# Moving the feed-forward weight loads from the ScalarE DMA queue to the SyncE DMA queue

## Chip, cores and metric

One Trainium2 chip, all 8 cores. Each core runs the same program on its own 2,048 of the 16,384 tokens; nothing is exchanged between cores. The metric is the device time in microseconds of the slowest core.

## What is computed

A transformer layer with attention over the 16 heads of one token, then a feed-forward block with ternary weights. Both blocks are wrapped as x + layernorm(block(layernorm(x))).

```python
def _quantize(w):
    gamma = jnp.mean(jnp.abs(w))
    return jnp.clip(jnp.round(w / (gamma + EPS)), -1.0, 1.0)
# attention: qkv = x @ W_qkv; scores over heads of one token; softmax; @ v; @ W_out + b_out
x = x + _layernorm(attn(_layernorm(x)))
# feed-forward, D = 2048, FF = 5632
x1 = _layernorm(x) @ _quantize(w1).T
x2 = _layernorm(x) @ _quantize(w2).T
hidden = sigmoid(x1) * x2
x = x + _layernorm(hidden @ _quantize(w3).T)
```

## The kernel before

Each core holds 2,048 tokens and works on them in two chunks of C = 1024. In order of time: chunk 0 goes through layernorm, QKV (`_phase_qkv`), attention, output projection (`_phase_wout`) and the residual (`_phase_y_ln_resid`); then chunk 1 does the same while `_quant_step` turns w1, w2 and w3 into ternary bf16 copies in HBM (`qw1T`, `qw2T`, `qw3T`); then `_phase_ffn` runs for chunk 0 and for chunk 1. The change is inside `_phase_ffn`.

The order of work is written out by hand. A `Builder` keeps one instruction list for each of the five sequencers (`sync` is SyncE, `scalar` ScalarE, `tensor` TensorE, `vector` VectorE, `gpsimd` GpSimd). `b.emit(engine, ...)` appends an instruction to that engine's list, and `b.wait_free` and `b.wait_ready` append semaphore waits to it. Each list is executed strictly in order, DMA issues among the rest: a DMA issue stands behind every wait and every instruction that was appended to the same list before it. `wait_free(ring, buffer)` waits until the last reader of the buffer is done, `wait_ready` until its last writer is.

`_phase_ffn` has three parts for each chunk:

- **The w1/w2 part** (lines 1038 to 1123). Twenty-two steps `mc`, each of 256 hidden columns. In a step, `wi = 0` multiplies by a band of w1 and `wi = 1` by a band of w2. A band is 1 MB and is loaded by two DMAs of 512 KB (lines 1070 to 1074). For each `wi` there are 4 groups (`mt`, `sub`) of 16 accumulating matmuls (line 1089), so 64 matmuls a band and 128 a step. After each w1 group ScalarE takes the sigmoid out of PSUM (line 1100); after each w2 group VectorE multiplies sigmoid and PSUM into `hid` (line 1117). w1 groups alternate between PSUM buffers `pbig` 0 and 1, w2 groups between `pbig` 2 and `pscore` 0. In chunk 0 each of w1 and w2 has a single SBUF buffer (`bandw1b` and `bandw2a`, keys `bandS`), since the others are still taken; in chunk 1 each has two (`bandw1a`/`bandw1b`, `bandw2a`/`bandw2b`).
- **The w3 part** (lines 1128 to 1191). Sixteen steps `dc`, each with a band of w3 of 1.4 MB, four DMAs of 352 KB (lines 1145 to 1149) into one half of the double buffer `band3`, then two groups of 44 matmuls (line 1168). `band3` lies over `bandw1a`, `bandw1b` and most of `bandw2b`, so its loads wait until those are no longer read. VectorE casts the result (line 1180) and GpSimd stores it to `yscr`. In chunk 0 at `dc == 1` the token matrix of chunk 1 is fetched by `_ffn_t2f_load`: 16 transposing DMAs on the sync list (line 1001), each waiting for the last w1/w2 matmul of chunk 0.
- **The tail** (lines 1208 to 1250). Eight row tiles: a transposing DMA from `yscr` on the sync list (line 1218), statistics and normalization on VectorE with two small ScalarE activations (lines 391 and 396), the residual (line 1240), and a store from GpSimd. The transposes alternate between two buffers, so from the third on each waits for VectorE to have read the tile two earlier (line 409).

Ahead of the feed-forward of chunk 0 stands `_phase_y_ln_resid(chunk=1)`, built in the same way: eight transposing DMAs on the sync list (line 764), and two layernorms for each tile with their ScalarE activations. `_ffn_t2f_load(0)` stands on the sync list ahead of it.

In the kernel before, all loads of w1, w2 and w3 bands are on the `scalar` list, between the ScalarE activations:

```python
for mc in range(NMC):
    for wi in range(2):
        ring = "scalar"
        ...                       # wait_free / wait_ready on ring, 2 DMAs on ring
        # 4 groups: 16 matmuls on tensor, then for wi == 0 a sigmoid on scalar
```

Of the kernel before, what the change touches and what calls it, by code (L numbers as in the profile page):

```python
# [236 lines left out]
def _build_all(b, ctx):  # L237
# [59 lines left out]
    for chunk in range(2):  # L297
        _phase_ffn(b, ctx, chunk)
        if b.dbg == "of":
            _dump_dram(b, ctx, "yscr", g("yscr")); return  # L300
        if b.dbg == "hid":
            _dump(b, ctx, "hid", g("hid")); return
        if b.dbg == "t2f":
            _dump(b, ctx, "t2f", g("t1f")); return
# [687 lines left out]
def _ffn_t2f_load(b, ctx, chunk):  # L992
    t2f = ctx["t1f"]
    act2 = ctx["act2scr"]
    b.wait_ready("sync", ("act2", chunk, 0))
    b.wait_ready("sync", ("act2", chunk, 1))
    for f in range(KD):
        b.wait_free("sync", ("t1f", f))
        b.emit("sync", lambda e, d=t2f[:, f * C:(f + 1) * C],
               s=act2[chunk * C:(chunk + 1) * C, f * 128:(f + 1) * 128]:  # L1000
               e.dma_start_transpose(out=d, in_=s),
               inc="dTf", inc_k=16)
    setm = ("dTf", b.pc["dTf"])
    for f in range(KD):
        b.produced(("t1f", f), setm)
    b.produced("t2f", setm)


def _phase_ffn(b, ctx, chunk):
# [27 lines left out]
    last_w1w2_mm = None  # L1037
    for mc in range(NMC):
        for wi in range(2):
            ring = "scalar"  # L1040
            if chunk == 0:
                dsem = f"dBS{wi}"
                bkey = ("bandS", wi)
                bandbuf = (ctx["bandw1b"], ctx["bandw2a"])[wi]
            else:
                dsem = f"dB{wi + 1}{mc % 2}"
# [80 lines left out]
    src3 = ctx["qw3T"].rearrange("(k p) m -> p k m", p=128)  # L1127
    for dc in range(NDC):
        b3 = ("band3", dc % 2)
        ring, dsem = (("scalar", "dB3a") if dc % 2 == 0 else ("scalar", "dB3b"))  # L1130
        b.wait_free(ring, b3)
        b.wait_free(ring, ("band", 0, 0))
        b.wait_free(ring, ("band", 0, 1))
        b.wait_free(ring, ("band", 1, 0))
        b.wait_free(ring, ("band", 1, 1))
        b.wait_free(ring, ("bandS", 0))
        b.wait_free(ring, ("ofin", 0))
        b.wait_free(ring, ("ofin", 1))
        b.wait_free(ring, ("xstg", 0))
        b.wait_free(ring, ("xstg", 1))  # L1140
        b.wait_ready(ring, "qwT3_done_0")
        b.wait_ready(ring, "qwT3_done_1")
        base3 = (dc % 2) * MFF * 128
        mlast = None
        for g4 in range(4):
            mlast = b.emit(ring, lambda e,
                           d=band3[:, base3:base3 + MFF * 128].rearrange("p (k m) -> p k m", m=128)[:, g4 * 11:(g4 + 1) * 11, :],
                           s=src3[:, g4 * 11:(g4 + 1) * 11, dc * 128:(dc + 1) * 128]:
                           e.dma_start(out=d, in_=s), inc=dsem, inc_k=16)
        b.produced(b3, mlast)  # L1150
        if chunk == 0 and dc == 1:
            _ffn_t2f_load(b, ctx, 1)
            ctx["_t2f_loaded_1"] = True
        for sub in range(2):
            mg = dc * 2 + sub
            pb = mg % 4
            pbuf = ("pbig", pb)
            b.wait_free("tensor", pbuf)
            b.wait_ready("tensor", b3)
            for k in range(MFF):  # L1160
                b.wait_ready("tensor", ("hid", k))
            mm = None
            for k in range(MFF):
                mm = b.emit("tensor", lambda e, p=pbig[pb][:],
                            w=band3[:, base3 + k * 128:base3 + (k + 1) * 128],
                            r=hid[:, k * C + sub * 512: k * C + sub * 512 + 512],
                            st=(k == 0), sp=(k == MFF - 1):
                            nc.tensor.matmul(p, w, r, start=st, stop=sp),  # L1168
                            inc="sT" if k == MFF - 1 else None)
            b.produced(pbuf, mm)  # L1170
            if sub == 1:
                b.consumed(b3, mm)
            if dc == NDC - 1 and sub == 1:
                for k in range(MFF):
                    b.consumed(("hid", k), mm)
            b.wait_ready("vector", pbuf)
            osl = ("ttok", mg % 2)
            b.wait_free("vector", osl)
            m_e = b.emit("vector", lambda e, d=ttok[:, (mg % 2) * D:(mg % 2) * D + 512],
                         s=pbig[pb][:]: nc.vector.tensor_copy(d, s), inc="sV")  # L1180
            b.consumed(pbuf, m_e)
            b.produced(osl, m_e)
            b.wait_ready("gpsimd", osl)
            b.wait_free("gpsimd", "yscr")
            m_w = b.emit("gpsimd", lambda e,
                         d=yscr[dc * 128:(dc + 1) * 128, sub * 512:sub * 512 + 512],
                         s=ttok[:, (mg % 2) * D:(mg % 2) * D + 512]:
                         e.dma_start(out=d, in_=s), inc="dYw", inc_k=16)  # L1188
            mj = b.join("gpsimd", [m_w])
            b.consumed(osl, mj)  # L1190
            out_wr.append(m_w)
# [101 lines left out]
```

How the kernel before makes its waits and increments, by code:

```python
            def wrapped(e, fn=fn, sem=sem, k=inc_k):  # L62
                fn(e).then_inc(sem, k)
# [7 lines left out]
    def wait(self, eng, sem_name, val):  # L71
        if val is None or val <= 0:
            return
        w = self.waited[eng]
        if w.get(sem_name, 0) >= val:
            return
        w[sem_name] = val
        sem = self.sem(sem_name)
        self.streams[eng].append(lambda e, s=sem, v=val: e.wait_ge(s, v))
        self.meta[eng].append(("w", sem_name, val))
```

## Time and profile before

| | us |
|---|---|
| median of three runs | 4797.99 |
| the three runs | 4756.2, 4797.99, 5081.45 |
| profiled execution, time | 4762.08 |
| profiled execution, span of the slowest core (core 6) | 4760.5 |
| span of the fastest core (core 5) | 4728.0 |
| TensorE matmul busy, share of span | 3069.1 (64%) |
| ScalarE busy | 1060.1 (22%) |
| VectorE busy | 1357.9 (29%) |

The span counts from the core's first to its last instruction. A busy time is the time in which at least one instruction of that engine is running; matmuls overlap, so their single durations are longer than their spacing. The granted clock is a share of 2.4 GHz: 1.00 is the upper level, 0.50 the lower (1.2 GHz). A row of the timeline joins successive instructions of one kind; "x64" says how many, and the bracket says how long the engine had been idle before and what ended that. "SPq" and "ACTq" are the SyncE and ScalarE sequencers issuing DMAs; a DMA row's duration is that of the issue, and the landing time counts from issue to completion.

### The profile page before, as it was taken

The page shows a single profiled execution, that of the slowest core. Times are in us where ns is not written, and L with a number is a line of the kernel's source. Part 1 is how long each engine was busy: PE and PEld are TensorE (multiplying, and loading weights), DVE is VectorE, ACT ScalarE, POOL GpSimd, SP SyncE. Part 2 cuts the span into 40 slices and gives each one's busy share as a digit, 9 for nine tenths or more (in the row PEclk, how much of TensorE's full clock was granted, in tenths as well). Part 3 has the DMA queues.
Part 4 walks back from the last instruction along what each step waited for, and adds up shares of the span by engine and source line. Part 5 has one row for each costly group of instructions (what it writes and reads, how often), then busy time and mean ns, then how long its engine had stood idle before and what let it go on. Part 6 is the DMA issues. An engine that isn't in the chain of part 4 may idle for free.

```text
span 4760.5 us, 41249 instructions; the slowest of 8 cores (4728.0 to 4760.5 us)
## 1 busy us (share of the span) xinstructions
PE 3069.1 (64%) x13836; PEld 1395.3 (29%) x13836; DVE 1357.9 (29%) x2375; ACT 1060.1 (22%) x1189; POOL 596.3 (13%) x1061
## 2 busy tenths in 40 slices
PE   2889611353199812630078888889938788788993
PEld 1333311121144311310033333334413333333441
DVE  3111122213666588755700000000040000000004
ACT  1666655432066623100000000000000000000000
POOL 1111111221033233323100000000000000000000
PEclk9987855676599955865589889989979899888996
DMA  7888744786399776898522222245452222223445
GB/s 144 266 263 263 236 152 151 219 279 201 116 301 299 262 227 199 260 233 230 163 71 53 58 67 53 53 102 103 88 168 53 68 57 53 64 61 65 88 86 159
DMA packets 735120, 718.06 MB, mean 151 GB/s; under 512 B 308160, under 2 KB 619584, under 8 KB 732736
## 3 DMA queue, kind: packets, MB, share of 16 engines
q0 software_dynamic: 120976, 438.37, 28.9%
q10 hardware_dynamic: 368768, 151.02, 13.2%
q1 hardware_dynamic: 245168, 126.03, 10.9%
q8 instruction: 114, 1.87, 0.2%
q14 instruction: 94, 0.77, 0.1%
HBM read 545.43 MB, written 157.29 MB: 148 GB/s over the span
## 4 chain that ended last, share of the span: by engine, by line
PE 49%; DMA 26%; DVE 13%; issue 6%; ACT 3%; SPq 1%; ACTq 1%; DVEq 0%; POOL 0%; POOLq 0%
PE pbig L1089 21%; PE pbig L1168 10%; DMA wsf<-wqkv 8%; PE pbig L530 6%; PE pscore L1089 6%; DMA qw3T<-ttok 5%; DMA wsf<-wout 4%; DMA bandw2a<-qw2T 4%; PE pscore L1168 3%; DVE stats L376 3%; DVE ttok L973 2%; DVE xcst L964 1%; DMA bandw2b<-qw2T 1%; PE pbig L716 1%; DVE xcst L959 1%
## 5 line engine op out<-in xcount | busy, mean ns | idle before, releaser
L530 PE MATMUL pbig<-t1f,wsb 128*128 128x512 bf16 x3072 | 725.5, 401 | 98.8 <-DVE wsb L486 91.1
L1089 PE MATMUL pbig<-t1f,bandw1b 128*128 128x512 bf16 x2112 | 463.2, 380 | 325.6 <-DMA bandw1b<-qw1T 325.6
L1168 PE MATMUL pbig<-hid,band 128*128 128x512 bf16 x2112 | 460.3, 380 | 10.1 <-DMA band<-qw3T 9.1
L530 PEld LDWEIGHTS pbig<-t1f,wsb 128*128 128x128 bf16 x3072 | 310.9, 102 | 513.0 <-issue 234.9
L1089 PE MATMUL pbig<-t1f,bandw2a 128*128 128x512 bf16 x1056 | 305.8, 455 | 205.7 <-DMA bandw2a<-qw2T 205.7
L1100 ACT ACTIVATE sigst<-pbig 128x512 bf16<-128x512 f32 x176 | 105.1, 597 | 1429.2 <-PE pbig L1089 1429.2
L1117 DVE TENSOR_TENSOR hid<-sigst,pbig 128x512 bf16<-128x512 bf16 x88 | 60.5, 687 | 1242.5 <-PE pbig L1089 1242.5
L1089 PEld LDWEIGHTS pbig<-t1f,bandw1b 128*128 128x128 bf16 x2112 | 207.1, 98 | 576.5 <-issue 328.8
L716 PE MATMUL pbig<-t1f,wsb 128*128 128x512 bf16 x1024 | 263.3, 424 | 127.3 <-DVE wsb L486 111.8
L660 PE MATMUL pmix<-wtb,vtb 128*128 128x128 bf16 x256 | 37.4, 300 | 466.8 <-DVE wtb L649 465.1
L1188 POOL DMA_DIRECT2D yscr<-ttok x64 | 34.6, 541 | 2192.1 <-issue 1637.6
L1168 PEld LDWEIGHTS pbig<-hid,band 128*128 128x128 bf16 x2112 | 206.9, 98 | 261.2 <-issue 13.5
L973 DVE TENSOR_TENSOR ttok<-xcst 128x1024 bf16<-128x1024 bf16 (+1 forms) x280 | 185.3, 662 | 255.1 <-DMA qw3T<-ttok 124.5
L1089 PE MATMUL pscore<-t1f,bandw2a 128*128 128x512 bf16 x1056 | 238.7, 379 | 0.0
L1089 PEld LDWEIGHTS pbig<-t1f,bandw2a 128*128 128x128 bf16 x1056 | 116.8, 113 | 389.4 <-issue 311.4
L669 ACT ACTIVATE t1f<-pmix 128x512 bf16<-128x512 f32 x64 | 156.9, 2451 | 324.9 <-PE pmix L660 324.9
L486 DVE CAST wsb<-wsf 128x1024 bf16<-128x1024 f32 x128 | 88.8, 697 | 483.1 <-DMA wsf<-wqkv 399.5
L1089 PE MATMUL pbig<-t1f,bandw1a 128*128 128x512 bf16 x704 | 155.5, 382 | 72.7 <-DMA bandw1a<-qw1T 72.7
L716 PEld LDWEIGHTS pbig<-t1f,wsb 128*128 128x128 bf16 x1024 | 107.5, 107 | 282.4 <-issue 198.6
L391 ACT ACTIVATE lntmp<-mv,epsc 128x1 f32<-128x1 f32 x64 | 18.8, 294 | 723.3 <-DVE mv L382 710.4
L541 ACT ACTIVATE qg<-pbig 128x512 bf16<-128x512 f32 x64 | 150.5, 2358 | 102.7 <-PE pbig L530 102.7
L541 ACT ACTIVATE vg<-pbig 128x512 bf16<-128x512 f32 x64 | 150.3, 2352 | 94.6 <-PE pbig L530 94.6
(89 smaller groups left out, 3155.7 us busy)
## 6 DMA issues: line engine op xcount, KB each, us to landing
xstg<-w POOLq DMA_DIRECT2D x222, 512.0 KB, 6.7
wsf<-w POOLq DMA_DIRECT2D x124, 512.0 KB, 6.2
ttf<-w POOLq DMA_DIRECT2D x100, 512.0 KB, 8.7
wsf<-wqkv SPq DMA_DIRECT2D x192, 256.0 KB, 6.9
band<-qw3T ACTq DMA_DIRECT2D x128, 352.0 KB, 5.8
bandw1b<-qw1T ACTq DMA_DIRECT2D x66, 512.0 KB, 7.0
bandw2a<-qw2T ACTq DMA_DIRECT2D x66, 512.0 KB, 5.0
xcF<-w POOLq DMA_DIRECT2D x50, 512.0 KB, 8.3
```

The costliest lines, as they stand in the source:

```text
L376: s=src_tile_ap[:, j * 512:(j + 1) * 512]: nc.vector.bn_stats(d, s),
L486: nc.vector.tensor_copy(d, s), inc="sV")
L530: nc.tensor.matmul(p, w, r, start=st, stop=sp),
L541: nc.scalar.activation(d, s, AF.Copy, scale=sc), inc="sS")
L669: nc.scalar.activation(d, s, AF.Copy), inc="sS")
L716: nc.tensor.matmul(p, w, r, start=st, stop=sp),
L959: nc.vector.tensor_scalar(d, s_, hg, None, ALU.is_gt), inc="sV")
L973: nc.vector.tensor_sub(d, a, gg), inc="sV")
L1089: nc.tensor.matmul(p, w, r, start=st, stop=sp),
L1100: s=pbig[pb][:]: nc.scalar.activation(d, s, AF.Sigmoid),
L1117: nc.vector.tensor_mul(d, a, p), inc="sV")
L1168: nc.tensor.matmul(p, w, r, start=st, stop=sp),
```

## The change

Every band load of the feed-forward block, w1, w2 and w3, in both chunks, is appended to the `sync` list and no longer to the `scalar` list, together with the waits in front of it. Sizes, buffers, semaphores, the wait conditions and the order of the loads among themselves are unchanged. The position of a load in the whole program text is unchanged too, so on the sync list a load stands behind whatever was appended there earlier: the transposes of lines 764, 1001 and 1218.

```diff
@@ -1037,7 +1037,7 @@
     last_w1w2_mm = None
     for mc in range(NMC):
         for wi in range(2):
-            ring = "scalar"
+            ring = "sync"
             if chunk == 0:
                 dsem = f"dBS{wi}"
                 bkey = ("bandS", wi)
@@ -1127,7 +1127,7 @@
     src3 = ctx["qw3T"].rearrange("(k p) m -> p k m", p=128)
     for dc in range(NDC):
         b3 = ("band3", dc % 2)
-        ring, dsem = (("scalar", "dB3a") if dc % 2 == 0 else ("scalar", "dB3b"))
+        ring, dsem = (("sync", "dB3a") if dc % 2 == 0 else ("sync", "dB3b"))
         b.wait_free(ring, b3)
         b.wait_free(ring, ("band", 0, 0))
         b.wait_free(ring, ("band", 0, 1))
```

## Rows read from the trace of the kernel before

**Rows 1.** Waits, whole span, TensorE at line 1089: total us, times, longest us.

```profile
PE pbig L1089 <- DMA bandw1b<-qw1T: 325.6, 1, 325.6
PE pbig L1089 <- DMA bandw2a<-qw2T: 205.7, 33, 6.9
PE pbig L1089 <- DMA bandw1a<-qw1T: 72.7, 1, 72.7
PE pbig L1089 <- DMA bandw2b<-qw2T: 68.6, 11, 6.5
```

**Rows 2.** Windows of chosen stretches, core 6: busy times, then granted clock, DMA share, GB/s.

```profile
1480.00:1650.00 170.00, 165.28 (x772) 74.55 (x769) 96.66 (x134) 114.92 (x50) 53.40 (x91) 1.00 0.86 292
2393.00:2700.00 307.00, 255.69 (x1088) 110.38 (x1088) 22.00 (x32) 22.78 (x37) 0.00 (x0) 0.90 0.21 56
3190.00:3495.00 305.00, 304.05 (x1408) 137.71 (x1408) 22.11 (x32) 0.00 (x0) 16.76 (x31) 1.00 0.51 108
```

**Rows 3.** Timeline of one w1/w2 step in chunk 0: start us, duration us, what.

```profile
2517.99 0.60 ACT L1100 ACTIVATE sigst<-pbig 128x512 bf16<-128x512 f32 x1 [2.86 <-PE pbig L1089]
2518.07 1.00 ACTq L1074 DMA_DIRECT2D bandw2a<-qw2T  x2
2519.16 2.85 ACTq L1074 DMA_DIRECT2D bandw1b<-qw1T  x2
2524.01 4.96 PE L1089 MATMUL pbig<-t1f,bandw2a 128*128 128x512 bf16 x16 [6.23 <-DMA bandw2a<-qw2T]
...
2539.17 13.98 PE L1089 MATMUL pbig<-t1f,bandw1b 128*128 128x512 bf16 x64
```

**Rows 4.** Timeline at the start of the feed-forward block, chunk 0.

```profile
2336.24 23.75 SPq L764 DMA_TRANSPOSE ytokB<-yscr  x3
...
2384.60 0.20 ACT L396 ACTIVATE rstd<-lntmp 128x1 f32<-128x1 f32 x1
2384.94 1.01 ACTq L1074 DMA_DIRECT2D bandw1b<-qw1T  x2
2392.97 15.98 PE L1089 MATMUL pbig<-t1f,bandw1b 128*128 128x512 bf16 x64 [325.62 <-DMA bandw1b<-qw1T]
2398.67 1.28 ACT L1100 ACT_TABLE_LOAD   x1 [13.87 <-PE pbig L1089]
2415.21 6.44 PE L1089 MATMUL pbig<-t1f,bandw2a 128*128 128x512 bf16 x16 [6.25 <-DMA bandw2a<-qw2T]
```

**Rows 5.** Timeline from the w1/w2 to the w3 part, chunk 0.

```profile
3190.06 25.39 SPq L1001 DMA_TRANSPOSE t1f<-act2scr  x16
3190.93 28.65 PE L1168 MATMUL pbig<-hid,band 128*128 128x512 bf16 x132 [1.01 <-DVE hid L1117]
3219.42 9.66 PE L1168 MATMUL pscore<-hid,band 128*128 128x512 bf16 x44
```

**Rows 6.** Timeline from the tail of chunk 0 to the start of chunk 1.

```profile
3498.70 49.54 SPq L1218 DMA_TRANSPOSE ytokB<-yscr  x8
3558.64 0.20 ACT L396 ACTIVATE rstd<-lntmp 128x1 f32<-128x1 f32 x1
3558.88 1.38 ACTq L1074 DMA_DIRECT2D bandw1a<-qw1T  x2
3567.71 15.71 PE L1089 MATMUL pbig<-t1f,bandw1a 128*128 128x512 bf16 x64 [72.72 <-DMA bandw1a<-qw1T]
```

**Rows 7.** Timeline from the w1/w2 to the w3 part, chunk 1.

```profile
4360.34 3.62 PE L1089 MATMUL pscore<-t1f,bandw2b 128*128 128x512 bf16 x16
4364.10 10.65 ACTq L1149 DMA_DIRECT2D band<-qw3T  x8
4373.06 17.32 PE L1168 MATMUL pbig<-hid,band 128*128 128x512 bf16 x71 [9.10 <-DMA band<-qw3T]
```

**Rows 8.** DMA issues (KB, us to landing); landings and an issue of line 1001.

```profile
wsb<-wqkvb SPq DMA_DIRECT2D x48, 512.0 KB, 5.6
DMA to landing us min/median/max: 3.7/8.4/23.7
2067.48 70.83 SPq L1001 DMA_TRANSPOSE t1f<-act2scr  x16
```

## Prediction

> **What bounds the kernel now.** I read the waits of TensorE first, because it is the busiest engine, then the windows by stage, then the timeline at each place where TensorE stands still in the feed-forward block. The waits show four entries at the w1/w2 matmuls [rows 1]. Two are single and long: 325.6 us before the first band of chunk 0 and 72.7 us before the first of chunk 1. Two are many and short: 33 waits for `bandw2a` and 11 for `bandw2b`, 44 in all, 274.3 us together, so 6.23 us each. There are 22 steps in each chunk, so every w2 band is waited for and, but for the first of a chunk, no w1 band ever is.
>
> The timeline of one step tells why [rows 3]. The two DMAs of the w2 band are issued at 2518.07, 0.08 us after the fourth sigmoid of that step has begun; in the program text that load stands right behind that sigmoid on the scalar list. The w1 matmuls have just ended when the load is issued, and TensorE idles 6.23 us until it lands. The load of the next w1 band follows at 2519.16 and has the whole w2 half to land in, which is why it costs nothing. In chunk 0 the buffer of w2 was free one half step earlier, and in chunk 1 (two buffers) earlier still. So the wait is due to the place in the list, not to a buffer and not to bandwidth: in this stretch the DMA share is 0.21, against 0.86 in the QKV stage [rows 2].
>
> Each stall also costs clock. The granted clock is 0.90 on average in the w1/w2 part and 1.00 in the w3 part, which has no such gaps [rows 2]. Undisturbed, 64 matmuls take 13.8 us: from 2539.17 a row of 64 ends at 2553.15, and the last of them is still in the pipeline when the next could start. By the w3 row, 132 matmuls take from 3190.93 to 3219.42, the next row's start, 28.49 us or 0.2158 us each [rows 5]. So a band is 13.81 us and a step 27.62 us. Measured, chunk 0's w1/w2 part lasts from 2392.97 [rows 4] to 1.01 us before 3190.93 [rows 5], 796.95 us, or 36.22 us a step. The 8.60 us above 27.62 are 6.23 of wait and 2.37 of lower clock after it (2415.21 shows one such group of 16 matmuls, 6.44 us for what takes 3.45 at full clock [rows 4]; 2524.01 a milder one of 4.96 [rows 3]).
>
> **The change, part by part.**
>
> *Steady state of the w1/w2 part.* On the sync list nothing but other loads stands between two band loads. The w2 load of step mc waits for the last w2 matmul of step mc-1 (chunk 0, single buffer) and then has the w1 half of step mc, 13.81 us, to land. Its duration has rows: 2518.07 to 2524.01 is 5.94 us from the first issue to the first matmul [rows 3], and the slowest first load is 2384.94 to 2392.97, 8.03 us [rows 4]. The w1 load likewise gets the w2 half. 13.81 against 5.9 to 8.0 leaves 5.8 us at the least, so both are hidden by matmuls; if that cover went, each would cost 6 us plus 2.4 us of clock, what it costs now. In chunk 1 the two buffers double the room. The SP queue as such is no slower by what rows there are: its 512 KB loads of `wsb` landed in 5.6 us in the median while the DMA engines were at 0.86 [rows 2, 8]. Leaving out the 44 stalls and their clock gives 22 x 8.60 = 189 us in each chunk before edges. What stands next behind the removed wait is TensorE itself: a sigmoid takes 0.60 us for every 3.45 us of matmuls [rows 3].
>
> *ScalarE's list* loses the issues (1.00 and 2.85 us a step [rows 3]) and their waits. Nothing on the path waits for that, so it counts zero; it is spare time of an engine that is busy 22.78 of 307 us [rows 2].
>
> *Start, chunk 0.* Before, the first load stands behind the last activation of the residual phase (2384.60 + 0.20) and is issued at 2384.94 [rows 4]. On the sync list it stands behind the last transpose of line 764, whose issue ends at 2336.24 + 23.75 = 2359.99. With the same 8.0 us the first matmul starts at 2368.0. But two w1 groups fill `pbig` 0 and 1 and the third needs a sigmoid, and ScalarE's sigmoids still stand behind its activation at 2384.60. With the table load of 1.28 and one sigmoid of 0.60 the third group can start at 2384.80 + 1.88 = 2386.7. TensorE is idle from about 2377 to there and falls back to the lower clock, so the third group takes 5.7 us (2392.97 to 2398.67, the first group now [rows 4]) and the fourth 3.45: the w1 half ends at 2395.8. Then w2 follows without a wait, 13.81, then 21 steps of 27.62, 580.0. End at 2989.6, against 3189.92 now: gain 200.3 us.
>
> *w3 part, chunk 0.* Bands 0 and 1 are issued, as now, when the last w1 matmul is done (line 1136), 13.8 us before the part begins; the same two bands took 8.96 us, from 4364.10 to 4373.06, in chunk 1 [rows 7]. Hidden. But band 2 now stands behind the 16 transposes of line 1001, which wait for the last w1/w2 matmul and took 25.39 us to issue [rows 5]. Before, band 2 could be issued after one step of w3, 88 matmuls or 19.0 us, beside the transposes on the other queue. It is needed after two steps, 38.0 us. Now it is issued at 25.4 or later and lands 9 us later at 34.4 (room: 3.6 us). No row shows a load behind transposes on one queue. Lower bound: the transposes go faster alone, nothing lost. Upper bound: the same 16 transposes once took 70.83 us, beside quantization traffic [rows 8]; band 2 would land at 79.8, 41.8 us late, and with 2.4 us of clock cost 44 us. I take 1 us, since the near row is the 25.39, which was itself measured with band 2 under way beside it. Bands 3 to 15 wait for buffers as before and have 19.0 us each.
>
> *Between the chunks.* The first load of chunk 1 is issued at 3558.88 behind the last activation of the tail (3558.64) [rows 6]. On the sync list it stands behind the last transpose, issued by 3498.70 + 49.54 = 3548.24. With the same 8.8 us to the first matmul it gains 10.6 us. ScalarE is done with the tail at 3558.84, before the first group ends (3557.1 + 5.4), so no sigmoid is late here. The load now follows a transpose in its queue, which may cost up to the 3.7 us of the shortest transpose [rows 8]; I take 1 us.
>
> *w1/w2 part, chunk 1.* Now 3567.71 [rows 6] to 4363.96 [rows 7], 796.3 us. After: 22 x 27.62 = 607.6, and the first band's lower clock, 15.71 against 13.98, 1.7 [rows 3, 6], 609.3. Gain 187.0 us.
>
> *w3 part, chunk 1, and tail.* Band 0 overlaps the last w2 band, so the 9.10 us wait [rows 7] stays on either queue. No change.
>
> **Sum.** 200.3 - 1 + 10.6 - 1 + 187.0 = 395.9 us. Against the profiled execution's own 4762.1 us that gives 4366 us. That execution lies 0.75% below the median of the three runs (4798.0) and close to the lowest (4756.2). I forecast the undisturbed time and add 4 us for small joints that I can't see: **4370 us**.
>
> **The rivals.**
>
> *Clock falls under unbroken load* (chance 0.05). After the change TensorE would run some 910 us with hardly a gap (608 + 304), two to three times as long as any such stretch now. The matmuls of the feed-forward block would be 2 x 608 + 2 x 304 = 1824 us at full clock. If the granted clock over it were c, they would take 1824/c: the gain falls under 2% at c = 0.86 and the kernel is 2% slower at c = 0.79. Rows speak against it: 305 us of the w3 part with TensorE busy 304.05 us run at 1.00, and 170 us of the QKV stage, whose operands are dense random numbers, as well [rows 2]. At c = 0.81, about where the time would stand still, it would give 4366 + 428 = 4794 us. The Trainium skill ("TensorE: Matmul & The Clock Gate", Part 1, the note on the peak-current limiter) speaks for this rival: it says that once three cores of a die run dense matmuls the die drops to 13/16 of the clock and that 1.95 GHz should be budgeted for sustained all-core work. An estimate from that page's ratio is 4366 + 1824 x 3/13 = 4787 us. By that rule the w3 part would not stand at 1.00, as it does with all eight cores at work, so the trace disagrees so far.
>
> *Nothing moves* (0.02). All queues feed the same DMA engines, and if the w2 wait were a matter of transfer, not of the place in the list, another queue would not help: 4762 us. Against it stand the issue 0.08 us after the sigmoid and the DMA share of 0.21 [rows 2, 3]. The Trainium skill ("DMA: Bandwidth & Descriptors", section "Issuing engines are not separate DMA queues") states that DMAs started from several engines interleave on the same 16 and that only the sequencer's issue time is saved, usually small. By that sentence alone the 3.85 us a step would leave ScalarE, off the path, and the time would stay at 4762 us; it says nothing of what a load waits behind in its issuer's list, which is what I count.
>
> *Band 2 of w3 is late behind the transposes* (0.08): up to 44 us, so up to 4410 us. For it: the room is only 3.6 us. Against: it happens once, and the 25.39 us has contention in it.
>
> *Loads on the SP queue land too slowly* (0.02; the one that ends slower). Place: every step of chunk 0, single-buffered. If a band takes L us to land, a step takes L + 13.81 + 2.4 as soon as L exceeds 13.81. That equals today's 36.22 at L = 20.0; with chunk 1's gain kept (two buffers give 41 us of room), the whole kernel is slower only when 22 x (L - 20.0) exceeds 197 us, L above 29.0, and by 2% above 33.3. The longest landing on this queue in the trace is 23.7 us, a transpose under heavy traffic [rows 8]. Were both halves of each band to take that, one behind the other, L = 47.4, chunk 0 would lose 22 x 27.4 = 603 us, chunk 1 would gain nothing, and the time would be about 5350 us. Against: 5.6 us in the median for loads of that size on this queue [rows 8].
>
> **How the numbers follow.** My forecast has 0.83, with its own span of 4345 to 4405: the lower end is the start of chunk 0 without the stop for the sigmoid (12 us) and the small terms at zero, the upper end 0.75% above 4370, which is what the median stands above the profiled execution. With late w3 loads on top, the range is 4340 to 4435. What is left out is the rest of 0.09 and part of the joints. About 2% is what a measurement of this kernel can tell from no change. Forecast, late w3 loads and a third of the slower-clock case (a drop to 0.9 only) are faster by over 2%, 0.93; the clock near 0.81 and nothing moved give 0.05 within 2%; 0.02 slower.
>
> **What would show it.** In the profile after: the w2 bands gone from TensorE's waits; the w1/w2 stretches at granted clock 1.00 and 27.6 us a step; first w1/w2 matmul near 2368 with an idle of some 10 us before the third group; w3 of chunk 0 beginning near 2991 and no idle between its steps (an idle of up to 42 us at its third step is the late band); 62 us and not 72.7 between the chunks; 9 us still before the w3 part of chunk 1. The prediction is wrong if w2 waits remain at about 6 us (the list was not the cause), or if the clock column drops under 0.95 in these stretches while TensorE has no gaps.

## Result: faster by 8.1%

The ratio of the changed kernel to the kernel before is 0.919, 95% interval 0.915 to 0.924. Applied to the 4762.1 us of the profiled execution of before that is 4377 us (4356 to 4399); 4370 was forecast. The profiled execution of the changed kernel took 4407.2 us, the lowest run 4373.8 us. In about half of the executions of either kernel a die of the chip runs at a lower clock for much of the time, and since those are left out of the ratio, the median over all ten runs, 4535.9 us, is no measure of the change.

The waits of TensorE in the feed-forward block, changed kernel, core 5 (the slowest): total us, times, longest us.

```profile
PE pbig L1089 <- DVE nbias L402: 285.5, 1, 285.5
PE pbig L1089 <- DMA bandw1a<-qw1T: 65.3, 1, 65.3
PE pbig L1168 <- DMA band<-qw3T: 16.3, 2, 8.9
PE pbig L1089 <- ACT sigst L1100: 9.4, 1, 9.4
```

All 44 waits for w2 bands of [rows 1] are gone. The first row is the wait for the start. VectorE is named as its releaser, but the timeline below shows the first w1 load issued at 2351.36 and the matmuls starting 7.0 us later, so it is that load. New are a wait for a sigmoid, 9.4 us, and a second one for a w3 band.

Windows of the same core: busy times, then granted clock, DMA share, GB/s.

```profile
2420.00:2700.00 280.00, 280.00 (x1299) 126.97 (x1298) 28.18 (x41) 23.92 (x40) 0.00 (x0) 1.00 0.27 76
3650.00:3955.00 305.00, 305.00 (x1415) 138.31 (x1414) 30.24 (x44) 26.31 (x44) 0.00 (x0) 1.00 0.25 70
3980.00:4100.00 120.00, 120.00 (x553) 54.24 (x552) 8.30 (x12) 0.00 (x0) 6.48 (x12) 0.99 0.40 88
4120.00:4320.00 200.00, 200.00 (x763) 82.89 (x762) 11.76 (x17) 0.00 (x0) 9.17 (x17) 0.81 0.31 67
```

TensorE is busy without a gap in the w1/w2 stretches of both chunks, at clock 1.00 where [rows 2] had 0.90. The last row is another matter: in the w3 part of chunk 1 the clock of this core stands at 0.81, below the upper level of 2.4 GHz and well above the lower of 1.2 GHz. More on that below.

The start, and two steps of chunk 0, same core (timeline; rows left out are the residual phase and the rest of the step).

```profile
2348.31 2.84 SPq L764 DMA_TRANSPOSE ytokB<-yscr  x1
2351.36 1.02 SPq L1074 DMA_DIRECT2D bandw1b<-qw1T  x2
...
2358.32 9.65 PE L1089 MATMUL pbig<-t1f,bandw1b 128*128 128x512 bf16 x32 [285.52 <-DVE nbias L402]
...
2374.83 0.20 ACT L396 ACTIVATE rstd<-lntmp 128x1 f32<-128x1 f32 x1
...
2375.18 1.28 ACT L1100 ACT_TABLE_LOAD   x1
...
2377.32 8.70 PE L1089 MATMUL pbig<-t1f,bandw1b 128*128 128x512 bf16 x32 [9.35 <-ACT sigst L1100]
...
2385.86 3.62 PE L1089 MATMUL pbig<-t1f,bandw2a 128*128 128x512 bf16 x16
...
2399.67 13.98 PE L1089 MATMUL pbig<-t1f,bandw1b 128*128 128x512 bf16 x64
2399.97 0.98 SPq L1074 DMA_DIRECT2D bandw2a<-qw2T  x2
...
2413.48 3.62 PE L1089 MATMUL pbig<-t1f,bandw2a 128*128 128x512 bf16 x16
```

The w2 band is now issued at 2399.97, as soon as the w2 matmuls of the step before have ended, and has 13.5 us until it is read at 2413.48. In [rows 3] it was issued after the sigmoids and read 5.9 us later, with TensorE waiting.

### The profile page after: what moved, and what is told of

The parts are those of the page before. It is cut to its first block, busy times and chain, and to the rows that moved or that the text cites. A ratio compares the mean times of both kernels' runs of the same rounds, so it can differ in the third digit from the quotient of the medians.

```text
span 4405.6 us, 41332 instructions; the slowest of 8 cores (4337.8 to 4405.6 us)
## 1 busy us (share of the span) xinstructions
PE 3003.0 (68%) x13836; PEld 1383.5 (31%) x13836; DVE 1356.9 (31%) x2375; ACT 1061.3 (24%) x1189; POOL 596.3 (14%) x1061
## 4 chain that ended last, share of the span: by engine, by line
PE 52%; DMA 22%; DVE 14%; issue 6%; ACT 4%; SPq 1%; DVEq 0%; POOL 0%; ACTq 0%; POOLq 0%
PE pbig L1089 20%; PE pbig L1168 11%; DMA wsf<-wqkv 9%; PE pbig L530 7%; PE pscore L1089 7%; DMA qw3T<-ttok 5%; DMA wsf<-wout 4%; PE pscore L1168 4%; DVE stats L376 3%; DVE ttok L973 2%; DVE xcst L964 1%; PE pbig L716 1%; DVE wsb L486 1%; DVE sums L592 1%; ACT ttf L844 1%
## 5 line engine op out<-in xcount | busy, mean ns | idle before, releaser
L530 PE MATMUL pbig<-t1f,wsb 128*128 128x512 bf16 x3072 | 721.2, 399 | 98.1 <-DVE wsb L486 93.3
L1168 PE MATMUL pbig<-hid,band 128*128 128x512 bf16 x2112 | 491.9, 398 | 16.3 <-DMA band<-qw3T 16.3
L660 PE MATMUL pmix<-wtb,vtb 128*128 128x128 bf16 x256 | 37.4, 300 | 467.6 <-DVE wtb L649 466.0
L716 PE MATMUL pbig<-t1f,wsb 128*128 128x512 bf16 x1024 | 256.0, 414 | 144.2 <-DVE wsb L486 125.0
L1089 PE MATMUL pbig<-t1f,bandw2a 128*128 128x512 bf16 x1056 | 238.7, 379 | 0.0
L1089 PE MATMUL pbig<-t1f,bandw1a 128*128 128x512 bf16 x704 | 156.1, 383 | 65.3 <-DMA bandw1a<-qw1T 65.3
L391 ACT ACTIVATE lntmp<-mv,epsc 128x1 f32<-128x1 f32 x64 | 18.8, 294 | 707.5 <-DVE mv L382 694.2
L1180 DVE CAST ttok<-pbig 128x512 bf16<-128x512 f32 x48 | 33.2, 691 | 472.5 <-PE pbig L1168 472.5
```

## Experiments

All kernels below are edits of one of the two kernels, and each was timed against the kernel before on the same chip.

### The changed kernel once more

> The changed kernel once more, for a second trace. My theory: TensorE's 44 waits for w2 bands are gone and a w1/w2 step takes 27.6 us in both chunks at a granted clock of 1.00; before the w3 part of chunk 0 TensorE waits 7 to 8 us for the first w3 band. The first trace had a granted clock of 0.81 on two cores (4 and 5) in the last 227 us. If that comes of the denser load of the changed kernel, this trace has such a stretch in its feed-forward block too, at some 40 us of cost on a core. If it is chance, it is gone here, and the slowest core is near 4370 us.

Ratio 0.918 (0.912 to 0.925), slowest core 4370.5 us. Windows of that core, core 3:

```profile
2700.00:2966.00 266.00, 266.00 (x1234) 120.54 (x1232) 26.80 (x39) 22.69 (x38) 0.00 (x0) 1.00 0.28 76
3980.00:4280.00 300.00, 297.57 (x1371) 134.60 (x1372) 21.44 (x31) 0.00 (x0) 16.19 (x30) 0.99 0.39 87
```

The w1/w2 part is as in the first trace, and the w3 part of chunk 1 has its clock of 0.99. The stretch at 0.81 is not a fixed part of the changed kernel.

### Is it the queue or the place in the list?

All loads on ScalarE, but those of a step ahead of its sigmoids (compared with the kernel before):

```diff
     for mc in range(NMC):
+        keys = []
         for wi in range(2):
             ring = "scalar"
             ...                      # waits and the two DMAs of the band
             b.produced(bkey, mlast)
+            keys.append((bkey, bandbuf))
+        for wi in range(2):
+            bkey, bandbuf = keys[wi]
             for mt in range(2):      # matmuls, sigmoids, products
```

> All loads stay on the ScalarE list, but the w2 load of a step is put ahead of the four sigmoids of that step. Theory (the place in the list made the stall): w2 waits gone, steps of 27.6 us at clock 1.00; 4762 - 2 x 189 = 4373 to 4385 us, ratio to before about 0.92; start of chunk 0 and the gap between the chunks (72.7 us) unchanged. Rival (the SyncE queue itself is what helped, being faster or empty): the waits of 6.2 us stay, 36.2 us a step, about 4762 us.

Ratio 0.919 (0.916 to 0.921), the same as the change's; lowest run 4385.4 us. One step, timeline of core 5:

```profile
2501.00 13.98 PE L1093 MATMUL pbig<-t1f,bandw1b 128*128 128x512 bf16 x64
2501.30 1.00 ACTq L1075 DMA_DIRECT2D bandw2a<-qw2T  x2
...
2514.81 3.62 PE L1093 MATMUL pbig<-t1f,bandw2a 128*128 128x512 bf16 x16
...
2515.25 1.00 ACTq L1075 DMA_DIRECT2D bandw1b<-qw1T  x2
```

The load is issued at the same point of the step as on SyncE, 0.30 us after the w1 matmuls begin, and TensorE waits for nothing. So the gain does not need the other queue at all. The Trainium skill ("DMA: Bandwidth & Descriptors", section "Issuing engines are not separate DMA queues") says that DMAs share the same 16 engines whichever engine started them, and this case agrees: a second queue brought no more than the first (0.919 both times), and below, a reload on one queue slows the loads on the other. The second rival of the prediction went further and took from that page that nothing would move. It failed, because the place in the list decides when a transfer may begin.

The opposite: loads on SyncE, but each w2 load also waits for the fourth sigmoid of its step.

```diff
+            if wi == 1:
+                b.wait(ring, m_sg[0], m_sg[1])
             src_r = wT[wi].rearrange("(k p) m -> p k m", p=128)
```

> The changed kernel (loads on SyncE), but each w2 load also waits for the fourth sigmoid of its step, which is where the ScalarE list issued it. Theory (only the moment of issue matters): TensorE waits about 6.2 us for each w2 band again, 36.2 us a step, granted clock 0.90; 4370 + 2 x 189 = about 4750 us, less the 20 to 30 us of the earlier starts. Rival (the SyncE queue as such is what helps): the waits stay away or are much shorter than 6 us.

Ratio 1.012 (1.005 to 1.019): the whole gain is gone, and the time is within 2% of that of the kernel before. Timeline of core 0:

```profile
2502.09 0.99 SPq L1076 DMA_DIRECT2D bandw2a<-qw2T  x2
...
2507.91 6.55 PE L1091 MATMUL pbig<-t1f,bandw2a 128*128 128x512 bf16 x16 [6.70 <-DMA bandw2a<-qw2T]
...
2539.52 0.98 SPq L1076 DMA_DIRECT2D bandw2a<-qw2T  x2
```

This step takes 2539.52 - 2502.09 = 37.4 us. From the first w2 group of chunk 0 at 2396.40 to the last but one at 3139.47 there are 20 steps of 37.15 us, against 36.10 in the kernel before (core 6, 21 steps from 2415.21 to 3173.28). The waits are 6.8 and not 6.3 us, since here the load waits until the sigmoid has ended, and in the kernel before it was issued 0.08 us after its start; the other 0.5 us is clock. 44 x 1.05 = 46 us is most of the 72 us that the expectation of 4750 us missed (lowest run 4822 us). The rest lies in the last w2 band of each chunk, same core:

```profile
3170.43 4.49 ACTq L1206 DMA_DIRECT2D xb<-xbscr  x8
3171.04 0.98 SPq L1076 DMA_DIRECT2D bandw2a<-qw2T  x2
...
3189.85 5.23 PE L1091 MATMUL pbig<-t1f,bandw2a 128*128 128x512 bf16 x16 [19.70 <-DMA bandw2a<-qw2T]
```

Held until the last sigmoid, this load starts 0.6 us behind the reloads of the residual `xb` and lands only after 18.8 us; in chunk 1 the wait is 18.6 us. That is 12 to 13 us more than for the other bands, twice. What the reloads do in the changed kernel itself is shown further down. The loads of w2 are on SyncE in this kernel and the stall is back in full, so the moment of issue sets it and not the queue.

### Which loads have to move?

Only the w2 loads on SyncE (compared with the kernel before):

```diff
-            ring = "scalar"
+            ring = "sync" if wi == 1 else "scalar"
```

> The kernel before with the w2 loads alone on SyncE; w1 and w3 loads stay on ScalarE. Theory: the steady state needs no more than this, so 27.6 us a step and 2 x 189 us gained. The start of chunk 0 keeps its place behind the last activation (no gain of 20 us), the gap between the chunks stays 72.7 us, and the xb reload stays behind the w3 loads (no 10 us lost): 4762 - 378 = 4384 us. Rival (w1 loads gained as well in the steady state): the time stays well above, and TensorE waits for w1 bands.

The lowest run was 4388.1 us, against 4757.3 us of the kernel before on the same chip, 0.922. No interval stands behind that, and a second series was run.

> Once more the kernel before with the w2 loads alone on SyncE, since all eight cores of the first trace stood at a granted clock of 0.81 through the whole feed-forward block and no ratio came out. Theory as before: 27.6 us a step, start of chunk 0 and the gap of 72.7 us between the chunks unchanged, 4762 - 378 = 4384 us, ratio about 0.92. Rival (w1 loads gained in the steady state too): clearly above, with TensorE waiting for w1 bands.

Again no interval came out. The lowest run was 4396.0 us, against 4774.4 us of the kernel before on the same chip, 0.921. Waits of core 3, the slowest (4409.8 us):

```profile
PE pbig L1089 <- DMA bandw1b<-qw1T: 313.2, 1, 313.2
PE pbig L1089 <- DMA bandw1a<-qw1T: 75.4, 1, 75.4
PE pbig L1168 <- DMA band<-qw3T: 9.1, 1, 9.1
```

No wait for any band inside the parts is left, though w1 and w3 loads are on ScalarE. The extra w3 wait of the changed kernel is absent. The two edges have not gained: over the eight cores TensorE waits 300 to 313 us at the start (295 to 326 before) and 72.3 to 76.1 us between the chunks (68.9 to 72.7 before, 62.3 to 65.3 in the changed kernel). Moving w2 alone is nearly the whole gain in these times; no interval stands behind the small difference.

### The unforeseen w3 wait

The changed kernel, timeline of core 5, from the w1/w2 to the w3 part of chunk 0:

```profile
2966.46 5.06 ACTq L1204 DMA_DIRECT2D xb<-xbscr  x8
2966.47 23.60 SPq L1149 DMA_DIRECT2D band<-qw3T  x8
...
2987.35 30.75 PE L1168 MATMUL pbig<-hid,band 128*128 128x512 bf16 x132 [7.36 <-DMA band<-qw3T]
2990.64 25.75 SPq L1001 DMA_TRANSPOSE t1f<-act2scr  x16
3016.54 54.63 SPq L1149 DMA_DIRECT2D band<-qw3T  x16
```

In the kernel before, the eight reloads of `xb`, 4 MB, stood on the ScalarE list behind the w3 loads. With those gone, nothing holds them back, and they start within 0.01 us of the first w3 band. The issue of eight w3 DMAs takes 23.60 us, where in [rows 7] it took 10.65. In chunk 1 the reloads start at 3955.62 and the w3 loads, which there have to wait for the last w2 matmul, only at 3969.29; the wait of 9 us for them is that of before. Two runs tell the collision from a fault of SyncE's queue or of the transposes.

```diff
-        ring, dsem = (("sync", "dB3a") if dc % 2 == 0 else ("sync", "dB3b"))
+        ring, dsem = (("scalar", "dB3a") if dc % 2 == 0 else ("scalar", "dB3b"))
```

> The changed kernel with the w3 loads back on the ScalarE list, w1/w2 loads on SyncE. Theory: the 7.4 us wait before the w3 part of chunk 0 comes from the xb reload (8 x 512 KB), which on the ScalarE list no longer stands behind the w3 loads and now shares the DMA engines with the first two w3 bands. With w3 back ahead of it, the wait is gone and about 2 us of lower clock with it: 10 us less than the changed kernel. Rival (the transposes of line 1001 or the SyncE queue are at fault): also gone here, so this run alone does not tell them apart; the run with the xb reload on SyncE does.

```diff
     for i in range(NTT):
-        b.wait_ready("scalar", ("xpark_done", chunk))
-        b.wait_free("scalar", ("xb", i))
-        b.emit("scalar", lambda e, d=xb[:, i * D:(i + 1) * D],
+        b.wait_ready("sync", ("xpark_done", chunk))
+        b.wait_free("sync", ("xb", i))
+        b.emit("sync", lambda e, d=xb[:, i * D:(i + 1) * D],
```

> The changed kernel with the eight xb reloads moved to the SyncE list too, where they stand behind the w3 loads again. Theory (collision with the xb reload): the first w3 wait of chunk 0 falls from 7.4 us to under 1 us with the w3 loads still on SyncE, about 10 us less. Rival (w3 loads are slower on the SyncE queue): the wait of 7.4 us stays.

The first gave 0.915 (0.913 to 0.918), the second 0.914 (0.908 to 0.920). In both, all eight cores have a single w3 wait, that of chunk 1. The second, core 4, its w3 wait:

```profile
PE pbig L1168 <- DMA band<-qw3T: 9.0, 1, 9.0
```

and its timeline at the same place:

```profile
2986.82 12.34 SPq L1149 DMA_DIRECT2D band<-qw3T  x8
...
3000.47 24.38 SPq L1001 DMA_TRANSPOSE t1f<-act2scr  x16
3025.00 14.98 SPq L1149 DMA_DIRECT2D band<-qw3T  x5
```

With the w3 loads still on SyncE, the issue of eight takes 12.34 us again and the wait is gone. So it was the reload beside them. The ratios only agree with that: the cost of the collision, 8.5 us or 0.2%, is less than the width of the intervals, and it is the trace that shows the mechanism.

### Wait and clock, the two terms of the stall

The changed kernel with each w2 load held behind the third sigmoid:

```diff
+            if wi == 1:
+                b.wait(ring, m_sg[0], m_sg[1] - 1)
```

> The changed kernel with each w2 load held back behind the third sigmoid of its step, 3.45 us earlier than behind the fourth. It parts the two terms of the stall, wait and clock. Holding behind the fourth gave waits of 6.7 to 6.8 us. So the wait should be 3.3 us a step. Theory (a wait costs clock in proportion to nothing but its being long enough): if a wait of 3.3 us still costs 2.4 us of lower clock the step is 27.6 + 5.7 = 33.3 us and the time about 4370 + 44 x 5.7 = 4621 us; rival (short waits cost no clock): 30.9 us a step, granted clock 1.00, about 4515 us.

No interval came out. The lowest run was 4631 us (4774 for the kernel before on the same chip), against 4621 expected with a clock cost and 4515 without. Timeline of core 4:

```profile
2547.87 0.98 SPq L1076 DMA_DIRECT2D bandw2a<-qw2T  x2
...
2553.75 6.56 PE L1091 MATMUL pbig<-t1f,bandw2a 128*128 128x512 bf16 x16 [3.32 <-DMA bandw2a<-qw2T]
```

and its window, clock 0.91:

```profile
2500.00:2800.00 300.00, 267.49 (x1114) 115.77 (x1134) 23.80 (x35) 21.53 (x36) 0.00 (x0) 0.91 0.24 64
```

In these rows a wait of 3.3 us is followed by as slow a group of 16 matmuls, 6.56 us, as one of 6.7 us was (6.55). Both rows are near the worst of their kernel, so here are the means: from 2383.59 to 3093.19 this core has 21 steps of 33.79 us, which is 27.62 of matmuls, 3.4 of wait and 2.7 of lower clock. With the waits of 6.8 us above the clock term was 37.15 - 27.62 - 6.77 = 2.8 us, and in the kernel before, with 6.3 us, 2.2 us. Half the wait does not halve the clock term.

### A version that beats both

The largest idle time left is the one before the first w1 band. Most of it is the quantization of w3, which the w1/w2 part does not read.

```diff
-    _quant_step(b, ctx, 10 ** 9)      # ahead of _phase_y_ln_resid(chunk=1)
...
     for mc in range(NMC):
         ...
+        if chunk == 0:
+            _quant_step(b, ctx, 3)
```

(with the `xb` reload on SyncE as above)

> A version that goes further: xb reload on SyncE as before, and the 56 quantization jobs of w3 that are left after the output projection of chunk 1 are no longer done in one piece ahead of the feed-forward block, but three in each w1/w2 step of chunk 0, which does not read w3. With the w2 stalls gone the largest idle time of TensorE is that before the first w1 band, about 285 us. Theory: that idle time shrinks to the residual phase, some 90 us, the w1/w2 steps of chunk 0 stay at 27.6 us since VectorE needs about 7 of them for the three jobs; about 4353 - 300 = 4050 us. Rival: the jobs keep VectorE or the DMA queues so busy that w2 groups wait for their PSUM buffer, steps get longer than 30 us and 50 us or more of it are lost.

Ratio 0.881 (0.877 to 0.885), median 4200 us, lowest 4193 us. The wait before the first w1 band is 111.6 us on the slowest core, core 0, and the w1/w2 part of chunk 0 is as dense as in the changed kernel (the waits, then a window):

```profile
PE pbig L1088 <- DMA bandw1b<-qw1T: 111.6, 1, 111.6
```

```profile
2300.00:2700.00 400.00, 400.00 (x1855) 181.37 (x1854) 129.36 (x186) 35.22 (x59) 49.43 (x88) 1.00 0.55 165
```

VectorE is busy 129 of 400 us there and holds nothing up. The expectation of 4050 us was wrong in its own sum: the idle time could fall only from 285 to some 90 us, which is 195 us and not 300. It fell by 174 us, and the ratio fell from 0.914 (`xb` reload on SyncE alone) to 0.881, 158 us of 4762.

> As the version that quantizes w3 beside the w1/w2 steps of chunk 0, but with all 88 jobs of w3 there, four in each step, and none in the output projection of chunk 1. Theory: the output projection was held up by the jobs (TensorE busy 111.6 of 125 us) and by the queue of their transfers ahead of the residual phase (some 25 us between its last matmul and the first transpose of y); both shrink, 20 to 30 us less than the 4193 us of that version. Rival: four jobs a step are too many for the DMA engines or VectorE, w2 groups wait, and nothing is gained.

This one moved all 88 w3 jobs (four a step) and took them out of the output projection. It has no ratio, and its lowest run was 4252 us. In that execution cores 4 and 5 (4218 and 4250 us) had a granted clock of 0.92 from 3700 to 4000 us; the cores 0 to 3 took 4167 to 4188 us, where they took 4166 to 4195 in the version above. So nothing is gained and little is lost. The start comes sooner (99.9 us of wait on core 0 and not 111.6), but the last jobs now end after the w1/w2 part. On core 0 that part ends at 2786.0, the last store of a w3 job is issued at 2796.66, and the first w3 bands, which wait for it, at 2799.19. TensorE waits some 22 us for them on all eight cores, where it stood idle 1.0 us in the version above (timeline, core 0):

```profile
2808.50 29.99 PE L1167 MATMUL pbig<-hid,band 128*128 128x512 bf16 x132 [22.47 <-DMA band<-qw3T]
```

## Why the prediction was right, point by point

**The cause of the stall** was right, and it is shown from both sides: the same order on ScalarE's own list gives the gain, the old moment of issue on SyncE takes it away.

**Size of the steady state.** 27.62 us a step was forecast. From the first w2 group at 2385.86 to the end of chunk 0's w1/w2 part (2966.02 is the last step's first w2 group) there are 21 steps in 580.2 us, 27.63 each. The cover was a little smaller than the prediction says, since the slowest first load in its rows is 8.83 us ([rows 6]) and not 8.03, but 5.0 us of it were left. Forecast for the whole stretch of chunk 1: 609.3 us; measured from 3358.81 to 3969.17, 610.4 us.

**Start of chunk 0.** All steps of the sum came out, counted from the end of ScalarE's last activation in the residual phase (2384.80 in the forecast, 2375.03 here): first matmul 16.8 us ahead of it (16.7), third group 1.9 us behind it (2.3), first w2 group 11.0 us behind it (10.8).

**The late w3 band 2 behind the transposes.** The transposes took 25.75 us to issue, 25.39 in [rows 5]; the room of 3.6 us held on core 5. On cores 0 and 4 band 2 came 1.8 and 1.0 us late: there the transposes, behind w3 loads that the `xb` reload had slowed, started over 2 us after the w3 matmuls and took 29 us to issue. With the reload out of the way (`xb` on SyncE) they start 0.9 us ahead of the matmuls on core 4, and none of the eight cores waits for band 2. The 44 us of the upper bound did not come.

**Between the chunks.** 62 to 63 us were forecast, 65.3 us measured on core 5 (timeline):

```profile
3348.26 0.98 SPq L1074 DMA_DIRECT2D bandw1a<-qw1T  x2
3349.29 7.34 SPq L1074 DMA_DIRECT2D bandw2a<-qw2T  x2
...
3358.81 16.37 PE L1089 MATMUL pbig<-t1f,bandw1a 128*128 128x512 bf16 x64 [65.27 <-DMA bandw1a<-qw1T]
```

From issue to first matmul is 10.55 us. The forecast had 8.8 from core 6 and 1 more for the transpose ahead, and both were sized wrong. Core 6 was an exception: the other seven took 5.8 to 7.0 us in the kernel before. In the changed kernel all eight took 8.9 to 10.6 us, some 3 us longer in the mean, so that the gap shrank by 6.9 us in the mean (70.2 to 63.3) and not by 9.6. The w2 load one microsecond behind is not what delays it. With w2 held back (the runs behind the third and fourth sigmoid) the w1 load still took 9.7 to 10.4 us on the four cores I read. With all loads on ScalarE's list, where a w2 load follows just as closely but no transposes stand ahead, it took 7.1 and 7.2 us on two cores. Whether it is the queue behind the transposes or the tail's other transfers at that earlier moment, no run separates.

**Missed: the `xb` reload.** The step that failed is "ScalarE's list loses the issues; nothing on the path waits for that, so it counts zero". I looked for what waits for ScalarE and not for what had been waiting behind the w3 loads on its list. What the runs showed in its place is the collision above. Its price is 6.4 us of wait (7.36 where [rows 5] has 1.01) and, since the first 132 matmuls take 30.75 and not 28.65 us, 2.1 us of clock: 8.5 us.

**The slower clock.** The rival did not decide, but I left out a row that spoke for it. The windows of the kernel before, core 6, show a clock of 0.83 in the QKV stage of chunk 0, and in the stretch where TensorE is busy nearly throughout, so that no idle time lowers the mean, 0.81:

```profile
300.00:550.00 250.00, 216.25 (x826) 88.14 (x824) 35.69 (x51) 167.19 (x155) 41.66 (x76) 0.83 0.86 263
350.00:400.00 50.00, 49.49 (x190) 20.36 (x188) 7.63 (x11) 35.93 (x32) 9.60 (x18) 0.81 0.92 290
```

And in the first trace of the changed kernel two cores of eight lost clock in the w3 part of chunk 1. Windows of 4100 to 4200 us, cores 4, 5, 6 and 7:

```profile
4100.00:4200.00 100.00, 99.29 (x374) 41.44 (x381) 6.22 (x9) 0.00 (x0) 4.85 (x9) 0.81 0.35 73
4100.00:4200.00 100.00, 100.00 (x383) 41.44 (x381) 6.23 (x9) 0.00 (x0) 4.86 (x9) 0.81 0.35 75
4100.00:4200.00 100.00, 100.00 (x465) 45.32 (x464) 6.91 (x10) 0.00 (x0) 5.41 (x10) 1.00 0.40 86
4100.00:4200.00 100.00, 100.00 (x465) 45.36 (x464) 7.61 (x11) 0.00 (x0) 5.51 (x11) 1.00 0.42 86
```

The w3 part of chunk 1 took from 3978.06 to 4323.74 on core 5, 345.7 us, against 306.2 in chunk 0: about 40 us, which made it the slowest core. The Trainium skill ("TensorE: Matmul & The Clock Gate", Part 1, the note on the peak-current limiter) names a step to 13/16 of the clock, 0.81, and the value fits. Its rule that a whole die drops and stays there while dense work lasts does not fit this trace: cores 6 and 7 are of the same die and stand at 1.00, and all eight cores ran the w1/w2 parts at 1.00. Another trace does fit it: in the first one of the kernel with w2 alone on SyncE, all eight cores, on both dies, stand at 0.81 or 0.82 from 3700 to 4000 us, in the w1/w2 part of chunk 1, with TensorE busy throughout. What sets it off is open. The second trace of the changed kernel has none of it in the feed-forward block, so the change does not bring it by necessity; whether it makes it likelier these runs can't say.

**Sum on core 5.** Before, this core had 4728.0 us, now 4405.6: 322.4 us less. Stage by stage in its own two traces, where the forecast was worked out on core 6:

| stage | gain on core 5, us | forecast, us |
|---|---|---|
| ahead of the last activation of the residual phase (2354.46, now 2375.03) | -20.6 | 0 |
| from there to the end of chunk 0's w1/w2 part | 198.0 | 200.3 |
| w3 part of chunk 0 with the wait before it | -8.5 | -1 |
| between the chunks | 5.0 | 9.6 |
| w1/w2 part of chunk 1 | 188.4 | 187.0 |
| w3 part of chunk 1 (lower clock) | -40.0 | 0 |

The first row is a stage that the change does not touch. The two large terms, which carry the forecast, came within 2.3 us each. In the second trace, without the last row's loss, the slowest core had 4370.5 us. That the forecast of 4370 lies so near the 4377 of the ratio is in part luck all the same: some 10 us of cost were missed or sized too small, against 4 us that had been added for joints.

**The range.** The bounds don't follow from the terms named for them: 4370 less 12 us and the small terms is about 4350, not 4345, and 44 us on top of 4405 would be 4449, not 4435. The result is near neither.

## What to carry to other kernels

Where loads and compute share one engine's instruction list, look at what stands in the list just ahead of each load. A load whose buffer is free can still be late because it queues behind instructions that wait for other engines; issuing it earlier on the same engine cured that here as well as another queue did (0.919 both). And when work leaves a list, ask what had been held back behind it: it may start at once and collide with what you moved.

## What was unexpected of the hardware

- A wait of TensorE of 3.4 us in the mean cost as much clock afterwards as one of 6.8 us: 2.7 and 2.8 us a step.
- 4 MB of reloads started with 2.8 MB of w3 loads on the other queue stretched the issue of the latter from 10.65 us to 23.60 us.
- The same 4 MB, started 0.6 us ahead of a 1 MB load, kept TensorE waiting 19.7 us for it and not 6.8.
- A 1 MB load issued behind the transposes of the tail took 8.9 to 10.6 us to the first matmul; issued later on the other queue it had taken 5.8 to 7.0 on seven cores of eight.
- The granted clock of 0.81 held on two cores of a die while the two others stood at 1.00 under the same load, and in another trace on all eight cores.
